# Softmax denominators in four column tiles, and a seventh rough-score copy by ScalarE, in a cross-attention and expert kernel

## The reference

```python
q = (layernorm(x) @ Wq)   # 16 heads of 64
k, v = ctx @ Wk, ctx @ Wv
scores = einsum('bqhd,bkhd->bhqk', q, k) / 8
attn = softmax(scores, axis=-1)          # over 1601 keys
x = x + einsum('bhqk,bkhd->bqhd', attn, v) @ Wo + bo
x = x + experts(layernorm(x))            # top-k routing, gelu, gated sum
```

## Time and profile before

| | |
|---|---|
| median of three runs | 1372.5 us (1370.81 to 1372.57) |
| profiled execution, time | 1379.77 us |
| profiled execution, span | 1378.0 us |
| PE busy in the span | 1297.1 us (94%) |
| DVE, POOL, ACT busy | 1021.9 (74%), 909.7 (66%), 797.3 us (58%) |

### The profile page before, as it was taken

One profiled execution on the slowest core, in us unless ns is written; L12 is line 12 of the kernel. 1 busy time (PEld: TensorE's weight loads), 2 busy tenths in 40 slices (PEclk: granted clock), 3 DMA queues, 4 the chain that ended last, 5 costly groups with the idle time before them and its releaser, 6 DMA issues. The chain is left out here.

```text
span 1378.0 us, 24851 instructions
## 1 busy us (share of the span) xinstructions
PE 1297.1 (94%) x8308; PEld 816.9 (59%) x8308; DVE 1021.9 (74%) x1708; ACT 797.3 (58%) x1061; POOL 909.7 (66%) x464
## 2 busy tenths in 40 slices
PE   6999999999999999999999999999999917999996
PEld 5655555555555555555555555555448906999996
DVE  5878877887887788788678877877987685655652
ACT  4556666666665666666566666666663215566653
POOL 2357977887786788778768877877695003355453
PEclk9999999999999999999999999999999957999998
DMA  9620010001001000100110020012304342454422
GB/s 274 220 93 17 17 56 17 17 25 57 24 17 57 18 17 24 57 16 24 43 32 17 17 64 17 17 53 72 112 31 169 132 127 95 124 137 107 101 37 28
DMA packets 76824, 88.84 MB, mean 64 GB/s; under 512 B 11771, under 2 KB 56604, under 8 KB 76700
## 3 DMA queue, kind: packets, MB, share of 16 engines
q1 hardware_dynamic: 69916, 78.32, 17.3%
q0 software_dynamic: 6784, 8.94, 4.0%
HBM read 58.13 MB, written 27.99 MB: 62 GB/s over the span
## 5 line engine op out<-in xcount | busy, mean ns | idle before, releaser
L927 POOL TENSOR_TENSOR acc_p<-acc_p,x_in 128x1024 f32<-128x1024 f32 x192 | 488.0, 2542 | 135.0 <-ACT x_in L1024 128.1
L112 DVE TENSOR_REDUCE mx_part<-ps_m 128x1 f32<-128x512 f32 x552 | 363.3, 686 | 172.1 <-PE ps_m L81 171.2
L1024 ACT ACTIVATE x_in<-ps_s 128x1024 f32<-128x1024 f32 x384 | 380.3, 1024 | 99.7 <-PE ps_s L841 70.5
L855 PE MATMUL ps_o<-x_in,v 128*64 128x512 f32 x1664 | 406.2, 606 | 0.0
L830 PE MATMUL ps_s<-q,k 64*128 64x512 f32 x2496 | 384.8, 394 | 1.2 <-ACT x_in L1024 1.2
L830 PEld LDWEIGHTS ps_s<-q,k 64*128 64x128 f32 x2496 | 272.8, 185 | 41.2 <-ACT x_in L1024 7.7
L81 PE MATMUL ps_m<-k,q 64*128 64x512 f32 x736 | 215.6, 455 | 8.1 <-DVE mx_part L112 3.4
L855 PEld LDWEIGHTS ps_o<-x_in,v 128*64 128x64 f32 x1664 | 99.5, 136 | 180.6 <-issue 141.1
L81 PEld LDWEIGHTS ps_m<-k,q 64*128 64x128 f32 x736 | 100.5, 183 | 166.8 <-issue 110.5
L927 DVE TENSOR_TENSOR acc_d<-acc_d,x_in 128x1024 f32<-128x1024 f32 x96 | 166.3, 1732 | 5.2 <-ACT x_in L1024 4.9
L707 ACT ACTIVATE kept<-ps_m 128x512 f32<-128x512 f32 x184 | 109.6, 596 | 82.9 <-PE ps_m L81 82.9
(11 more groups left out here) (251 smaller groups left out, 1934.5 us busy)
## 6 DMA issues: line engine op xcount, KB each, us to landing
w_in<-in_w SPq DMA_DIRECT2D x16, 1024.0 KB, 5.0
v_st<-rec_scr SPq DMA_DIRECT2D x64, 128.0 KB, 2.9
o_scr<-v_st SPq DMA_DIRECT2D x32, 256.0 KB, 2.1
v<-v_scr SPq DMA_DIRECT2D x7, 832.0 KB, 5.2
v_scr<-c_in SPq DMA_DIRECT2D x10, 512.0 KB, 3.7
c<-o_scr SPq DMA_DIRECT2D x2, 1792.0 KB, 8.2
x_in<-in_x SPq DMA_DIRECT2D x4, 512.0 KB, 10.0
m_rows<-mx_t SPq DMA_DIRECT2D x128, 1.0 KB
```

Source lines behind the costliest of these rows:

```text
L112: dve.tensor_reduce(part[:, j // S.MF, j % S.MF:j % S.MF + 1], bank[:, 0:S.MC], AX.X, ALU.max).then_inc(done or G.rough_used[hd], 1)
L855: last = pe.matmul(ps_o[hd * HP:hd * HP + DH, :], v[b][:, s, hd * DH:(hd + 1) * DH], probs[:, g % RING, hd * QC:(hd + 1) * QC], start=(s = ...
L927: eng.tensor_tensor(acc, other, probs[:, (u * KT + t) % RING, :], ALU.add).then_inc(done, 1)
L1024: act.activation(probs[:, g % RING, :], ps_s[:, g % 2, :], ACT.Exp, bias=G.pad_bias[:, 0:1] if s == KT - 1 else 0.0, scale=SCALE).then_inc ...
```

## The change

`KEPT` gets job 8 as a seventh entry, so that ACT also copies head 1's rough scores of slot 4, after the exponentials of slots 3 and 4. With seven copies a unit the two buffers no longer start at the same one in every unit, so the buffer follows the running number (`kept_buffer`). The denominators are made by four matmuls of 32 output rows and 256 columns instead of two of 64 rows and 512 columns; the results stand in rows 0, 32, 64 and 96 of 256 columns. ACT copies 256 columns instead of 512, and one DMA instead of two brings them to the 16 partitions.

```diff
-KEPT = (0, 2, 5, 7, 9, 11)
+KEPT = (0, 2, 5, 7, 8, 9, 11)
...
+DEN_TILES = 4
...
+    DP, DQ = P // DEN_TILES, UQ // DEN_TILES
...
+        def kept_buffer(j, u):
+
+            return (len(KEPT) * (u - 1) + KEPT.index(j)) % 2
+
...
-                act.activation(kept[:, KEPT.index(j) % 2, :], ps_m[:, 1, :], ACT.Copy).then_inc(kept_made, 1)
...
+                act.activation(kept[:, kept_buffer(j, u), :], ps_m[:, 1, :], ACT.Copy).then_inc(kept_made, 1)
...
-                    rough_max(S, G, dve, kept[:, KEPT.index(j) % 2, :], hd, j, kept_read)
+                    rough_max(S, G, dve, kept[:, kept_buffer(j, u), :], hd, j, kept_read)
...
-            for b in range(2):
-                last = pe.matmul((ps_x if bank is None else bank)[b * HP:(b + 1) * HP, :], G.ones[:, 0:HP], acc_p[:, u % 2, b * QC:(b + 1) * QC],
-                                 start=True, stop=True)
+            for i in range(DEN_TILES):
+                last = pe.matmul((ps_x if bank is None else bank)[i * DP:(i + 1) * DP, 0:DQ], G.ones[:, 0:DP],
+                                 acc_p[:, u % 2, i * DQ:(i + 1) * DQ], start=True, stop=True)
             last.then_inc(den_ready, 1)
...
-            wait_for(act, den_moved, 32 * unit)
-            act.activation(den_sb[:], (ps_x if bank is None else bank)[:], ACT.Copy).then_inc(den_copied, 1)
+            wait_for(act, den_moved, 16 * unit)
+            act.activation(den_sb[:], (ps_x if bank is None else bank)[:, 0:DQ], ACT.Copy).then_inc(den_copied, 1)
...
-            for b in range(2):
-                sp.dma_start(den_c[8 * b:8 * b + 8, :], den_sb[b * HP:b * HP + 1, :]).then_inc(den_moved, 16)
+            sp.dma_start(den_c[:], den_sb[0:P:DP, :]).then_inc(den_moved, 16)
...
                     for s in group:
                         exponentials(u, s)
+                    if len(group) == 2:
+                        rough(u, group[1])
                     copies(u, group[-1])
```

More of the change, by code:

```diff
@@ L700, in kept_count, with act_rough @@
             return len(KEPT) * (unit - 1) + KEPT.index(j) - sum(k < MAHEAD for k in KEPT)
-        def act_rough(act, j, unit, count):
+        def kept_buffer(j, u):
+            return (len(KEPT) * (u - 1) + KEPT.index(j)) % 2
+        def act_rough(act, j, unit, count, u):
             if j in KEPT:
@@ L706, in act_rough, with dve_rough @@
                 act.wait_ge(rough_ready[1], count + 1)
-                act.activation(kept[:, KEPT.index(j) % 2, :], ps_m[:, 1, :], ACT.Copy).then_inc(kept_made, 1)
-        def dve_rough(dve, j, unit, count):
+                act.activation(kept[:, kept_buffer(j, u), :], ps_m[:, 1, :], ACT.Copy).then_inc(kept_made, 1)
+        def dve_rough(dve, j, unit, count, u):
             if j == 0:
@@ L879, in act_den @@
             act.wait_ge(den_ready, unit + 1)
-            wait_for(act, den_moved, 32 * unit)
-            act.activation(den_sb[:], (ps_x if bank is None else bank)[:], ACT.Copy).then_inc(den_copied, 1)
+            wait_for(act, den_moved, 16 * unit)
+            act.activation(den_sb[:], (ps_x if bank is None else bank)[:, 0:DQ], ACT.Copy).then_inc(den_copied, 1)
         def sp_den(sp, unit):
             sp.wait_ge(den_copied, unit + 1)
-            for b in range(2):
-                sp.dma_start(den_c[8 * b:8 * b + 8, :], den_sb[b * HP:b * HP + 1, :]).then_inc(den_moved, 16)
+            sp.dma_start(den_c[:], den_sb[0:P:DP, :]).then_inc(den_moved, 16)
         def dve_rec(dve, unit):
-            dve.wait_ge(den_moved, 32 * (unit + 1))
+            dve.wait_ge(den_moved, 16 * (unit + 1))
             dve.reciprocal(rec_c[:], den_c[:]).then_inc(rec_ready, 1)
@@ L1044, in rough @@
                     j, ahead = job
-                    act_rough(act, j, p * UNITS + u + ahead, (p * UNITS + u + ahead) * MJOBS + j)
+                    act_rough(act, j, p * UNITS + u + ahead, (p * UNITS + u + ahead) * MJOBS + j, u + ahead)
             for u in range(UNITS):
@@ L1070, in dve_pair @@
                     j, ahead = job
-                    dve_rough(dve, j, unit + ahead, (unit + ahead) * MJOBS + j)
+                    dve_rough(dve, j, unit + ahead, (unit + ahead) * MJOBS + j, u + ahead)
                 if s == REC_SLOT and not (first and u == 0):
@@ L2111, in build @@
             G.v_st = lasting("v_st", [P, 2, S.DI], F32)
-            G.den_sb = lasting("den_sb", [P, S.QC], F32)
+            G.den_sb = lasting("den_sb", [P, S.UQ // DEN_TILES], F32)
             G.den_c, G.rec_c = (lasting(n, [16, 2 * S.QC // 16], F32) for n in ("den_c", "rec_c"))
```

## The result

The changed kernel takes 1362.6 us (median of four runs, 1360.8 to 1363.5) against 1372.5 us, 10 us less. The profiled execution took 1360.8 us, its span 1359.0. Two more measurements gave 0.9926 (0.9910 to 0.9941) and 0.9924 (0.9911 to 0.9938), the first of them on a chip on which both kernels took 10 us longer.

The account below looks back on a forecast made before the run. PE was taken to bound attention; 28 units times (0.30 from the tiles + 0.13 from the lifted wait) plus 0.2 us gave 12.2 us, from 1372.5 to 1360.3 us. The range was 1355.3 to 1373.0 us.

Parts of the forecast that it names:

- group behind: PE from the rough scores after the denominators to the next values: 2.05 us expected, 2.19 before.
- What bounds: Attention, 100 to 940 us: PE bounds, busy 835.6 of 840 us, so time cut from its stream counts fully.
- Part 1: PE's denominators as four column tiles: block 0.56 us instead of 0.86, gain 0.30 us a unit.
- the change of form: PE between values and denominators: new cost of 0.09 us, plus 0.04 for weight load not hidden.
- single-file issue: Pessimistic case for the denominators: eight records issued one by one at 0.071 us each, gain only 0.09 us.
- Part 2: ACT copies head 1 of job 8 in idle time, 0.59 us at no cost, freeing PE of 0.13 us a unit.
- The hold: PE's rough scores behind the denominators wait for DVE's maxima of job 8 to free head 1's bank: 0.13 us a unit.
- what is next late: ACT's copy of job 9, needed by job 10's head 1, ends at 511.80, just about when PE takes the bank.
- The sum: 28 units times (0.30 + 0.13) give 12.0 us, plus 0.2 for four later denominator blocks: 12.2 us.
- (a): ACT's copy of job 9 gates PE, losing 0.43 us in 14 units: 1366.3 us; chance 0.08.
- (b): Denominator tiles run only two at a time, block 0.99 us: no change, 1372.5 us; chance 0.10.
- (c): Four denominator tiles run one after another, block 1.85 us against 0.86: slower, 1396.6 us; chance 0.06.

Follow-up runs that it names:

- four by 512: Changed kernel with each of the four denominator tiles streaming 512 columns instead of 256; 1.0014 of the time before the change.
- half-column experiment: Changed kernel with denominators from two 64-column matmuls of 256 columns, half the columns left out; 0.9879 of the time before the change.
- copy only: Kernel before plus ACT's copy of job 8 and the single DMA, still two column tiles of 64 by 512; 0.9994 of the time before.

## Why the prediction was right, and where it was off

The time forecast was 1360.3, measured 1362.6; 12.2 us forecast, 10.4 measured with an interval that ends at 12.1. The profile shows what was forecast: 1.10 us from the start of the last pass of the values to the rough scores (forecast 1.08, before 1.38), a group behind of 2.05, waits of ACT of 1.0 us (forecast 0.9). The last denominators of the stretch came 11 us earlier, not 12.

**What bounds:** right. PE's share stayed over 99% of the stretch, and 0.43 us added to its block in each unit (four by 512) came out as time.

**Part 1:** 0.30 us forecast, (0.96 + 1.77) - (0.57 + 1.86) = 0.30 measured. Its pieces hold too: the change of form with 0.13 to 0.14 (half-column experiment), the passes with 0.43. Within the first, the weight load was half of the 0.04 that I took. The low bound's single-file issue doesn't occur. The Trainium skill's rule that a new tiling mode drains TensorE ("TensorEngine Tiling (Array Packing)", Key Properties) agrees with the trace also between two column tilings: 0.09 us on entering. What TensorE does in this time no run shows.

**Part 2:** right in what it does, right in size, and wrong about the cause in the unit that I showed. The hold was 2.17 - 2.05, or 0.11 to 0.12 us, on the mean, forecast 0.13. In three of four units DVE makes it: in the earlier trace rows the two rough scores take 0.62 us from the first start to the last end, where undisturbed ones take 0.50, so head 1 comes 0.12 us late. But in the unit of the prediction they take 0.52, so DVE held PE for 0.02 us only. The rest of the 0.14 came from ACT's copy of job 9: it ended at 511.80, and PE's second rough score of job 10 started at 511.85, with the values another 0.10 us later than in an undisturbed group:

```profile
511.56 0.39 PE L81 MATMUL ps_m<-k,q 64*128 64x512 f32 x1
...
511.85 0.49 PE L81 MATMUL ps_m<-k,q 64*128 64x512 f32 x1
```

I had named that copy as what is next late, but not as a cause already at work. That the size agreed in this unit is luck: the two holds happen to be nearly alike. The gain came in these units too because the narrower copy of the denominators, which I had called off the path, lifts ACT's hold. It isn't off the path in a quarter of the units.

**The sum:** (0.29 + 0.12) x 27 is 11.1 us, and the steady stretch gave 10.9, where 27 x 0.43 had said 11.6. The step from denominators to denominators that crosses the first end of the loop body gained 0.04 us, the others 0.42 each. PE's rows behind this end, before and after:

```profile
436.64 0.69 PE L81 MATMUL ps_m<-k,q 64*128 64x512 f32 x2 [1.41 <-issue]
```

```profile
432.08 0.61 PE L81 MATMUL ps_m<-k,q 64*128 64x512 f32 x2 [1.81 <-issue]
```

I had not looked at that place; its longer pause and the fall of the clock behind it in some executions are what the sum left out. In exchange, the last four blocks gave more. From the 28th block to the first matmul of the output phase 1.2 us were won (934.4 to 1037.7 before, 923.3 to 1025.3 after): 0.4 by the 28th block itself, which the sum holds, and 0.8 by the four others, where I had counted 0.2 with a bound of 1.2. The largest of these, 0.50 us, is the one that a wait for DVE was to swallow. The wait stayed (0.58 us before, 0.53 after) but moved ahead with PE: DVE's work in front of it starts with a maximum that waits for ACT's copy, and so for PE, and from this maximum to PE's row it is 4.5 us in both kernels. So the total of the trace, 12.4 us up to the output phase, meets the forecast of 12.2 in part by luck, since a term too high and a term too low cancel.

**The rivals:** (a), ACT as the gate, doesn't occur in the changed kernel, but its mechanism is real: in a quarter of the units of the kernel before and of copy only. (b) and (c), tiles that don't run together, fell with four by 512.

## What to carry to other kernels

Before shortening a block on the bounding engine, look at when the buffer that the next instruction needs comes free: here a cut of 0.3 us gave nothing by itself, and 0.4 us with a 0.6 us copy on an engine that was idle just then. Count from start to start and compare the same group of instructions in two places, since a hold of 0.1 us did not show in the list of PE's waits. And see in the row itself which instruction was late: the unit taken as proof of DVE's hold was one of ACT's. A copy's price is its place in its engine's queue: the same copy behind the denominators cost 40 us.

## What the runs showed of the hardware

- Four column tiles of 32 with fp32 operands stream together at the rate of two tiles of 64: 0.22 us for a pass of 256 columns, 0.43 for 512.
- Going from the 64-column form to four tiles of the 32-column form costs PE 0.13 to 0.14 us, though both use all rows: 0.09 on entering, 0.02 of weight load, and the rest two further tiles that start 7 ns apart.
- Pauses of PE of 1.7 to 2.2 us at the end of a loop body were followed in five of eleven traces by a granted clock of 1.2 GHz for part of the next 7 us, at a cost of about 2 us, and pauses of 1.8 and 2.0 us in others were not. The longest pause differs from 1.3 to 2.2 us between kernels whose loop bodies differ slightly; what sets it stays open.
- A DVE addition of two 128x1024 fp32 tiles in SBUF takes 1.21 us with POOL idle and 2.12 with a POOL subtraction of 1.06 us beside it.
